# Sampling loop: step size, B and C spread by three row groups of TensorE from one product, and the softplus sum taken one step later

## The reference, cut to what matters

```python
xd = _dcn_sample(xc, offset)                       # bilinear sampling, 4 groups
xs = xd.reshape(Bn, C, L)
x_dbl = jnp.einsum('rc,bcl->brl', x_proj_w, xs)     # 8 rows for dt, 1 for B, 1 for C
dts, Bs, Cs = jnp.split(x_dbl, [DT_RANK, DT_RANK + D_STATE], axis=1)
dts = jnp.einsum('dr,brl->bdl', dt_w, dts)
delta = softplus(dts + dt_bias)
h = exp(delta * A) * h + delta * Bs * xs            # scan along the pixels
y = Cs * h + Ds * xs
out = einsum('bchw,oc->bohw', layer_norm(y), out_proj_w)
```

## Time and profile before

| | us |
|---|---|
| median of 3 runs (lowest, highest) | 2433.93 (2433.17, 2436.31) |
| the profiled execution | 2433.49 |
| its span, first to last instruction | 2431.7 |
| busy in the span: TensorE | 2121.9 |
| VectorE | 1832.2 |
| ScalarE | 1421.9 |
| GpSimd | 1421.0 |

### The profile page before, as it was taken

One profiled execution on the slowest core, in us unless ns is written; L12 is line 12 of the kernel. 1 busy time (PEld: TensorE's weight loads), 2 busy tenths in 40 slices (PEclk: granted clock), 3 DMA queues, 4 the chain that ended last, 5 costly groups with the idle time before them and its releaser, 6 DMA issues. The chain is left out here.

```text
span 2431.7 us, 28756 instructions
## 1 busy us (share of the span) xinstructions
PE 2121.9 (87%) x7363; PEld 1094.8 (45%) x7363; DVE 1832.2 (75%) x3128; ACT 1421.9 (58%) x2192; POOL 1421.0 (58%) x1305
## 2 busy tenths in 40 slices
PE   2998759898998999997988977798989799999798
PEld 2397435443553444433335954453345334444243
DVE  6555667499986999995755648566999589999754
ACT  1843454286885777773346437336778567777632
POOL 2233009498967999972322410475989399999532
PEclk9978879999999999998988979899999799999899
DMA  5000283500001122225810007433000011222344
GB/s 190 1 1 0 85 310 88 206 1 1 1 1 27 40 44 59 42 55 170 229 37 0 1 1 262 172 107 149 0 1 1 12 27 40 61 43 58 88 122 113
DMA packets 199340, 172.80 MB, mean 71 GB/s; under 512 B 72535, under 2 KB 175327, under 8 KB 195831
## 3 DMA queue, kind: packets, MB, share of 16 engines
q1 hardware_dynamic: 199159, 170.78, 24.5%
HBM read 81.69 MB, written 72.29 MB: 63 GB/s over the span
## 5 line engine op out<-in xcount | busy, mean ns | idle before, releaser
L948 POOL TENSOR_TENSOR BIG<-BIG 128x512 f32<-128x512 f32 x320 | 408.1, 1275 | 93.7 <-DVE BIG L856 74.6
L856 DVE TENSOR_TENSOR BIG<-PSUM,BIG 128x512 f32<-128x512 f32 x576 | 392.1, 684 | 63.4 <-PE PSUM L1067 36.8
L1139 DVE SCALAR_TENSOR_TENSOR PSUM<-BIG,VECS,PSUM 128x1024 f32<-128x1024 f32 x224 | 288.2, 1287 | 38.6 <-PE PSUM L2112 33.5
L1075 PE MATMUL PSUM<-BIG,CSTS 128*128 128x512 f32 x512 | 265.9, 600 | 0.0
L782 POOL TENSOR_TENSOR BIG<-TOEP,BIG 128x384 f32<-128x384 f32 x84 | 98.1, 1195 | 269.6 <-DVEq L1544 269.6
L2112 PE MATMUL PSUM<-BIG,WDW 128*128 128x512 f32 x512 | 234.2, 602 | 12.5 <-ACT BIG L2012 12.5
L1067 PE MATMUL PSUM<-BIG,SELB 120*128 120x512 bf16 x576 | 211.2, 385 | 19.3 <-issue 9.0
L2308 PE MATMUL PSUM<-BIG 128*128 128x381 f32 (+1 forms) x576 | 188.8, 491 | 12.9 <-DVE BIG L789 12.9
L1067 PEld LDWEIGHTS PSUM<-BIG,SELB 120*128 120x128 bf16 x576 | 55.1, 96 | 264.8 <-DVE BIG L856 163.2
L2112 PEld LDWEIGHTS PSUM<-BIG,WDW 128*128 128x128 f32 x512 | 97.8, 193 | 140.2 <-issue 118.0
L1785 POOL TENSOR_TENSOR BIG<-BIG 128x1024 f32<-128x1024 f32 x64 | 151.2, 2363 | 10.3 <-POOL BIG L1788 10.3
(11 more groups left out here) (363 smaller groups left out, 5070.3 us busy)
## 6 DMA issues: line engine op xcount, KB each, us to landing
spill<-X SPq DMA_DIRECT2D x18, 1024.0 KB, 6.8
back_spill<-BIG SPq DMA_DIRECT2D x32, 576.0 KB, 3.4
X<-x SPq DMA_DIRECT2D x32, 512.0 KB, 7.9
rows_spill<-X SPq DMA_DIRECT2D x64, 256.0 KB, 4.2
out<-BIG SPq DMA_DIRECT2D x64, 256.0 KB, 3.6
BIG<-rows_spill SPq DMA_DIRECT2D x28, 512.0 KB, 5.1
X<-back_spill SPq DMA_DIRECT2D x14, 896.0 KB, 12.6
BIG<-fc SPq DMA_DIRECT2D x8, 1024.0 KB, 9.8
```

The costliest lines, as they stand in the source:

```text
L856: dve.tensor_tensor(img(product_buffer(b, q)), img(PSUM[:, (k + q) % 2, :]), pch(c, XBASE, dy, dx), ALU.mult).then_inc(df_p, 1)
L948: pool.tensor_tensor(a, a, x, ALU.add).then_inc(df_add, 1)
L1075: pe.matmul(PSUM[:, ACC, :], ident, product_buffer(b, m), start=(m == 0), stop=(m == PE_SUMS - 1)).then_inc(df_acc, 1)
L1139: return dve.scalar_tensor_tensor(out=rows8(to), in0=strip(c, base, dy, dx), scalar=vc(weights, j), in1=rows8(acc), op0=ALU.mult, op1=ALU.add)
```

## The change

TensorE's three products from XS become one and three. WX has ten columns (dt rank, B, C) for each image, three times over, at rows 0, 32 and 64; ScalarE copies the 96 rows from PSUM to `AB`; then three products with 32 rows each (`WG`) spread the step size, B and C to the banks ZB, BB and CB. `WG` is loaded by six small DMAs that stand in SyncE's queue behind the image loads; the folding of x_proj and dt_w at set-up goes. VectorE's RL moves from the end of step c (tile c-1) to step c, ahead of p2, for tile c-2; UU times B and the scan move behind p4. ScalarE's DA moves to the front of its step, ahead of the hats, also for tile c-2. GpSimd's code is the same.

```diff
@@ VectorE
+                if on(-2):
+
+                    dve.wait_ge(sc_ln, after(T - 2))
+                    dve.wait_ge(sc_u, after(T - 3))
+                    dve.wait_ge(sc_da, after(T - 3))
+                    dve.tensor_tensor(RL, PSUM[:, ZB, :], AB, ALU.add).then_inc(sc_delta, 1)
                 product(2)
+                product(3)
+                if not far:
+                    product(4)
                 if on(-2):
 
                     dve.wait_ge(sc_u, after(T - 2))
-                    dve.wait_ge(sc_bc, after(T - 2))
+                    dve.wait_ge(sc_zbc, all_three(T - 2))
                     dve.tensor_tensor(PSUM[:, BB, :], UU, PSUM[:, BB, :], ALU.mult).then_inc(sc_bx, 1)
...
                 product(8)
-                if on(-1):
-
-                    dve.wait_ge(sc_ln, after(T - 1))
-                    dve.wait_ge(sc_u, after(T - 2))
-                    dve.wait_ge(sc_da, after(T - 2))
-                    dve.tensor_tensor(RL, PSUM[:, ZB, :], AB, ALU.add).then_inc(sc_delta, 1)
@@ ScalarE
+                if on(-2):
+
+                    act.wait_ge(sc_delta, after(T - 2))
+                    act.wait_ge(sc_h, after(T - 3))
+                    act.activation(DA, RL, ACT.Exp, scale=SM[:, 9:10]).then_inc(sc_da, 1)
...
                 if on(-1):
-                    act.wait_ge(sc_z, after(T - 1))
-                    act.activation(AB, PSUM[:, ZB, :], ACT.Abs, bias=vc("dt_b")).then_inc(sc_abs, 1)
-                    act.wait_ge(sc_abs, after(T - 1))
+
+                    act.wait_ge(sc_xd, after(T - 1))
+                    act.wait_ge(sc_delta, after(T - 2))
+                    act.activation(AB[0:3 * 32, :], PSUM[0:3 * 32, ZB, :], ACT.Copy).then_inc(sc_copied, 1)
+                if on(0):
+
+                    act.wait_ge(df_acc, summed(T, PE_SUMS - 1, PE_SUMS))
+                    act.wait_ge(sc_y, reuse(T))
+                    act.activation(XS[:, k, :], PSUM[:, ACC, :], ACT.Copy).then_inc(df_xs, 1)
+                if on(-1):
+                    act.wait_ge(sc_zbc, all_three(T - 1))
+                    act.activation(AB, PSUM[:, ZB, :], ACT.Abs, bias=vc("dt_b")).then_inc(sc_copied, 1)
+                    act.wait_ge(sc_copied, copied(T - 1, 1))
@@ TensorE
-                    pe.matmul(PSUM[:, ZB, :], WZ[:, :], XS[:, (k + 1) % 2, :], start=True, stop=True).then_inc(sc_z, 1)
+                    pe.matmul(PSUM[:, ZB, :], WX[:, :], XS[:, (k + 1) % 2, :], start=True, stop=True).then_inc(sc_xd, 1)
                 spread(6)
                 if not far:
                     add_up(3)
                 spread(7)
                 if on(-1):
-                    pe.matmul(PSUM[:, BB, :], WB[:, :], XS[:, (k + 1) % 2, :], start=True, stop=True)
+
+                    pe.wait_ge(sc_copied, copied(T - 1, 0))
+                    pe.wait_ge(sc_y, after(T - 2))
+                    settle(pe)
+                    for r, bank in enumerate((ZB, BB, CB)):
+                        rows = slice(r * 32, r * 32 + 32)
+                        pe.matmul(PSUM[:, bank, :], WG[rows, :], AB[rows, :], start=True, stop=True).then_inc(sc_zbc, 1)
                 spread(8)
-                if on(-1):
-                    pe.wait_ge(sc_y, after(T - 2))
-                    pe.matmul(PSUM[:, CB, :], WC[:, :], XS[:, (k + 1) % 2, :], start=True, stop=True).then_inc(sc_bc, 1)
```

More of the change, by code:

```diff
@@ L31 @@
 DT_RANK = 8
+XR = DT_RANK + 2
 PW = W + 2
@@ L135, in program @@
         CSTS = sb("CSTS", [P, NCST + P])
-        WQ, WK, WV, WPROJ, WIN, WZ, WB, WC = (sb(n, [P, P]) for n in
-            ("WQ", "WK", "WV", "WPROJ", "WIN", "WZ", "WB", "WC"))
+        WQ, WK, WV, WPROJ, WIN, WX = (sb(n, [P, P]) for n in ("WQ", "WK", "WV", "WPROJ", "WIN", "WX"))
+        WG = sb("WG", [3 * 32, P])
         WOUT2, GNE = sb("WOUT2", [P, P]), sb("GNE", [P, 2])
@@ L367, in program @@
         far_xs = sem("far_xs")
[L368 to L371, removed]
+        (sc_zbc, sc_copied, sc_exp, sc_ln, sc_delta, sc_u, sc_da, sc_bx, sc_h, sc_hc, sc_y, sc_cen, sc_proj, sc_sq, sc_var,
+         sc_lv, sc_rs, sc_t, sc_x, sc_xd) = (sem(n) for n in (
+            "sc_zbc", "sc_copied", "sc_exp", "sc_ln", "sc_delta", "sc_u", "sc_da", "sc_bx", "sc_h", "sc_hc",
+            "sc_y", "sc_cen", "sc_proj", "sc_sq", "sc_var", "sc_lv", "sc_rs", "sc_t", "sc_x", "sc_xd"))
         l3_xn = sem("l3_xn")
@@ L441, in parts_moved, with all_three, copied @@
             return pair * MOVES[n % 2] + SPREAD[n % 2] + (n // 2 + 1) * 64
+        def all_three(t):
+            return 3 * (t + 1) + CREDIT
+        def copied(t, n):
+            return 2 * t + (n + 1 + CREDIT)
         def strip_done(pair, c):
@@ L504, in _ @@
             sp.wait_ge(const_act, 3)
+            for s in range(2):
+                at, cols = s * XR, slice(s * C, (s + 1) * C)
+                sp.dma_start(WG[at:at + DT_RANK, cols], dts[:, 2 * C:3 * C]).then_inc(load, 16)
+                for r in (1, 2):
+                    row = r * 32 + at + DT_RANK + r - 1
+                    sp.dma_start(WG[row:row + 1, cols], cst[0:1, CST["one"][0]:CST["one"][0] + C]).then_inc(load, 16)
             sp.dma_start(rt_spill, RT).then_inc(rt_saved, 16)
@@ L585, in _ @@
                 pair_rows(PARTS3 - 2)
-                sp.wait_ge(sc_delta, pair * NT + (NT + CREDIT))
+                sp.wait_ge(sc_xd, pair * NT + (NT + CREDIT))
                 settle(sp)
@@ L882, in step @@
                                            ALU.mult, ALU.add).then_inc(sc_h, 1)
[L883 to L889, removed]
+                if far:
+                    if on(-1):
+                        if on(0):
+                            dve.wait_ge(df_acc, summed(T, PE_SUMS - 1, PE_SUMS))
+                        dve.wait_ge(df_add, summed(T - 1, POOL_SUMS - 1, POOL_SUMS))
+                        far_dve(dve, c - 1, (k + 1) % 2, reach)
+                    product(4)
                 if on(-2):
@@ L1045, in step @@
                 if on(-1):
-                    act.wait_ge(sc_delta, after(T - 1))
-                    act.wait_ge(sc_h, after(T - 2))
-                    act.activation(DA, RL, ACT.Exp, scale=SM[:, 9:10]).then_inc(sc_da, 1)
+                    act.wait_ge(sc_zbc, all_three(T - 1))
+                    act.activation(AB, PSUM[:, ZB, :], ACT.Abs, bias=vc("dt_b")).then_inc(sc_copied, 1)
+                    act.wait_ge(sc_copied, copied(T - 1, 1))
+                    act.activation(PSUM[:, ZB, :], PSUM[:, ZB, :], ACT.Relu, bias=vc("dt_b"))
+                    act.activation(AB, AB, ACT.Exp, scale=-1.0).then_inc(sc_exp, 1)
+                    act.wait_ge(sc_exp, after(T - 1))
+                    act.activation(AB, AB, ACT.Ln, bias=1.0).then_inc(sc_ln, 1)
             straight(act, pair, step)
@@ L1174, in _ @@
             dve.reg_mov(far_dve_turn, 0)
-            dve.wait_ge(load, 16 * 9)
-            for w in (WQ, WK, WV, WPROJ, WIN, WOUT, WZ, WB, WC):
+            dve.wait_ge(load, 16 * 8)
+            for w in (WQ, WK, WV, WPROJ, WIN, WOUT, WX, WG):
                 dve.memset(w[:, :], 0.0)
@@ L1211, in _ @@
                 dve.tensor_copy(WCONV[p:q, s, :], mt("conv", p, q))
-                xp = MAT["x_proj"][0]
-                for w, col in ((WB, DT_RANK), (WC, DT_RANK + 1)):
-                    dve.tensor_copy(w[p:q, p:q], MATS[p:q, xp + col:xp + col + 1].broadcast_to([C, C]))
+                dve.tensor_copy(WX[p:q, 0:3 * 32].rearrange("p (r m) -> p r m", r=3)[:, :, s * XR:(s + 1) * XR],
+                                mt("x_proj", p, q).unsqueeze(1).broadcast_to([C, 3, XR]))
                 dve.tensor_scalar(WOUT[p:q, p:q], mt("out_proj", p, q), vc("out_ln_g")[p:q], None, ALU.mult)
@@ L1251, in _ @@
             dve.wait_ge(const_pe, 1)
-            for s in range(2):
-                p, q = s * C, s * C + C
-                dve.tensor_copy(WZ[p:q, p:q], PSUM[p:q, 0, 0:C])
             dve.tensor_copy(OUTB[:, :], PSUM[:, 1, 0:1])
@@ L1827, in _ @@
             credit(act, l1_sq, sp_stage, sp_pixt, sp_exp, o_at)
-            credit(act, df_abs, df_hat, df_hi, df_mid, df_xs, sc_abs, sc_exp, sc_ln, sc_da, sc_sq, sc_lv, sc_rs)
-            act.wait_ge(load, 16 * 9)
+            credit(act, df_abs, df_hat, df_hi, df_mid, df_xs, sc_copied, sc_exp, sc_ln, sc_da, sc_sq, sc_lv, sc_rs)
+            act.wait_ge(load, 16 * 8)
             act.wait_ge(const_dve, 9)
@@ L2077, in _ @@
             credit(pe, sp_lgt, sp_tr, sp_fold, o_tr, o_mm, cv_mm)
-            credit(pe, df_w, df_acc, sc_z, sc_bc, sc_cen, sc_proj, sc_var)
+            credit(pe, df_w, df_acc, sc_xd, sc_zbc, sc_cen, sc_proj, sc_var)
             pe.reg_mov(far_pe_turn, 0)
             pe.reg_mov(far_pe_done, 0)
-            pe.wait_ge(load, 16 * 9)
+            pe.wait_ge(load, 16 * 8)
             pe.wait_ge(const_dve, 9)
-            pe.matmul(PSUM[:, 0, 0:C], DTS[:, 0:2 * C], DTS[:, 2 * C:3 * C], start=True, stop=True)
             pe.matmul(PSUM[:, 1, 0:1], PLAIN[:, :], vc("out_ln_b"), start=True, stop=True)
@@ L2392, in _ @@
```

(1 more changed line is left out.)

10 lines of the change are left out of this document (1 added, 9 removed).

## The result

The changed kernel takes 2589.76 us (median of 4 runs, 2587.84 to 2596.37) against 2435.12 us for the kernel before (4 runs, 2433.17 to 2436.57): a ratio of 1.064, 95% interval 1.0619 to 1.0662. The profiled execution took 2587.84 us, 154.35 more than the one before.

What follows compares the result with a forecast made beforehand. A loop from RL through UU and the transpose back to RL was to bound each step: 29 x 2.47 = 71.6, -1.3, +3.8, together 74.1 us a pair, 148.2 for two, on 2433.49: 2582 us, forecast 2565 to 2600 (66%).

Steps and rivals of the forecast that it cites:

- The loop: RL, UU, W9, hi to mid, transpose, spread(0), p0, next RL: 13.34 us a step against 10.87, 2.47 more.
- The 1.3 I took off the first step: First of a pair's 29 lengthened steps: 1.3 us less, as two VectorE output instructions (0.60 + 0.67) are missing.
- The ends: Last tile of each pair: scan waits for UU, later RL, copy and three products, estimated 2.1 + 0.6 + 1.1 = 3.8 us.
- TensorE's path: From add4 through WX, copy, three products, spread(8), p8 to p0: 9.9 us after RL's end, 0.3 before the transpose's way.
- the chain: UU, W9, hi to mid, transpose, spread(0), p0; 0.13 us slack before; without UU's wait on it, VectorE's 10.46 us a step.
- way (b): RL, UU, W9, add3, remainder, add4, WX, spread(6), p6, p7, three products, spread(8), p8, p0; named only after measuring.
- TensorE's relief: Rival: UU's wait is off the chain, the loop falls to VectorE's 10.46 us, about 2408 us; 5%.
- The products in turn: Rival: TensorE's three 32-row products take 2.58 us, 3.7 us more per step, about 2654 us; 8%.
- The price of 1.5 us: Rival of TensorE's clock falling to 1.2 GHz: 1.5 us per step hit, 2611 to 2669 us; 15%.
- way (a): The predicted way from RL to p0: UU, W9, hi to mid, transpose, spread(0), then p0 and the next RL.

Runs made afterwards that it cites:

- the run with the sum alone: Kernel before with RL and DA for tile c-2 one step later, BX product and scan behind p4, TensorE's products unchanged: 2585.69 us, ratio 1.0606.
- the run of the products alone: Kernel before with WX, the copy and the three 32-row products, while RL, DA, BX and scan keep their old places: 2610.48 us, ratio 1.0729.
- the run with the sum ahead of p0: Changed kernel with VectorE's RL of tile c-2 moved from ahead of p2 to ahead of p0: 2611.43 us, ratio 1.072.

## Why the prediction was right

The measured 2589.76 us lie 7.8 above the forecast of 2582 and inside its own 2565 to 2600.

**The loop** was right, step by step. From RL's end (1037.20 + 0.68 = 1037.88) in the step shown: to UU 0.08 (0.05 in the sum), UU and W9 2.31 (2.30), to hi 0.04 and hi to mid's end 3.88 (0.03 and 3.88), to the issue 0.30 (0.30), issue to spread(0) 3.10 (3.1 + 0.12), to p0 0.43 (0.42), p0 to RL 2.46 (2.46), RL 0.68. That is 13.28 us, predicted 13.34. The 29 long steps cost 73.0 us a pair where 71.6 - 1.3 were forecast. The 1.3 I took off the first step did not come: that interval took 13.99 us (14.12 in the second pair) at a mean granted clock of 0.88, and in it WX took 2.08 us behind a wait of 3.45. A few steps of 13.5 to 14.2 us, at a clock of 1.00, add some 2 us a pair; in the longest, spread(0) came 3.99 us after the transpose's issue instead of 3.10. The ends were 2.6 and 3.5 us, predicted 3.8, and 2.3 us outside the loops were not predicted. That the step came out is not luck; that the total lies as near as 7.8 us is in part, since a step forecast 0.06 us too long and ends forecast too long made up for some of what was missing.

**TensorE's path** was the term that was mis-sized. I gave it 0.3 us of slack; it has about 0.1. WX came 5.58 us after RL's end (5.55), the three at 7.94 (7.8), spread(8) at 9.00 (8.9), p8 at 9.43 (9.3), and p0 could follow at 10.03 (9.9), 0.11 ahead of the transpose's way at 10.14 (10.2). It did not move the sum, but it matters for the remedy: I wrote that taking UU's wait off "the chain" would bring VectorE's 10.46 us. There are two chains, both hang on UU, freeing either one leaves 13.1 or 13.3 us, and shortening both left 11.7.

**What would show it.** UU waits for RL in every step, by 3.0 us and not the 2 I gave, since nearly all of GpSimd's idle time of a step collects there (2.96 of 3.26 us in the step shown). spread(0) waits for the transpose. VectorE's idle time is 426 - 337.16 = 88.8 us in the first loop, 22.2 before, so 66.7 more where about 145 were forecast for the two loops. It lies ahead of p6, p7 and p8 (1.27, 0.39, 0.69) and hardly ahead of p0. I had named p0 or p6, and had written that I am wrong if p0 does not wait for the transpose: way (b), which holds VectorE up just before, leaves p0 only 0.11 us to wait, so this sign could not decide. The run with add3 and add4 ahead of UU does: with way (b) off UU, p0 waits 0.61 us and the step stays at 13.3. The three products took 1.06 us (1.08).

By the Trainium skill's page "TensorEngine Tiling (Array Packing)", section "Key Properties", a change of the tiling mode drains TensorE. No run here shows a drain by itself. Whatever it costs is inside the 1.06 us and the 0.31 between spread(7) and the first of the three, where a spread costs 0.22; the run with the products in turn, which changes the mode just as often, prices the row groups but not a drain.

**The rivals.** TensorE's relief counted for nothing: the run with the sum alone has the same time within the intervals. The products in turn are a real danger, at 14.87 us a step (14.55 predicted). In the changed kernel TensorE's clock fell at the beginning and the end of the loops, not in their middle, so the clock took its part in the first step of each pair. The price of 1.5 us that I gave to a step that is hit is not borne out for this loop. It holds where TensorE's queue behind p0 sets the step: 1.38 us in the run of the products alone, 1.3 to 1.4 in the run with the sum ahead of p0. In two runs in which way (a) or way (b) sets the step, a fall was hidden or nearly so: with add3 and add4 ahead of UU, steps at mean clocks of 0.87 to 0.91 between 840 and 1140 us took 13.28 to 13.55 us, those at 1.00 13.27 to 13.53; with the three in turn they took the same 14.87.

## What to carry to other kernels

When an instruction moves to a later place on its engine, list who waits for its result and what is queued behind the waiter; if one of these things feeds back to the moved instruction within one step, add up the way round, because that sum, if it exceeds the old step, is the new one, and idle capacity elsewhere does not shorten it. Then look for a second way round: two equal loops hide each other, and removing either one alone gains next to nothing (0.17 us a step at most here). A relieved engine is worth something only if its work, and not a wait within it, sets the step.

## What the runs showed of the hardware

Three float32 products of 32 rows and 512 columns took 1.06 us on three row groups and 2.77 us in turn on one, 0.92 each; a product of 128 rows took 0.86. So a product with a quarter of the rows costs no less time, and three row groups gave 2.6 of the 3 times that they could. In the run of the products alone the granted clock fell to 0.50 in nearly every second step, at a mean of 0.88 over those steps; in the changed kernel, with a wait of 1.74 us in each step, it stayed at 1.00 through the middle of the loop. What a fall costs depends on where it lies in the step: 1.38 us in the run of the products alone, next to nothing with the three in turn, where steps at 0.84 and at 1.00 both took 14.87 us. The transpose landed 3.1 us after its issue in the median, before (19 of them) as after (all 64), but the changed kernel's slowest took 6.4.
